# Building a graph's count matrix by ranges of 32 destinations, with paired comparisons and addresses on GpSimd

## The reference, cut to what matters

```
src = randint(40000, 0, 2500)
dst = int(2500 * uniform(40000) ** 2.0)      # then both sorted by dst
W   = zeros((256, 256)).at[src, dst].set(edge_weight)     # second layer; the last writer wins
out = segment_sum(alpha * h[src], dst)                    # attention, and the like for means
```

## Time and profile before

| | us |
|---|---|
| median of 3 runs | 2374.59 (2371.84 to 2375.01) |
| profiled execution, span | 2375.9 |
| counting stage, first to last matmul of line 571 | 41.6 to 335.6 |
| PE busy over the span | 1749.6 |
| VectorE busy | 1671.4 |
| ScalarE busy | 1385.3 |
| GpSimd busy | 334.5 |

### The profile page before, as it was taken

How to read it: one execution, slowest core, us unless ns; L and a number is a source line. 1 busy time by engine, 2 the same in 40 slices (tenths; PEclk the granted TensorE clock), 3 DMA queues, 4 the chain that set the end, 5 groups by cost and what they waited for, 6 DMA issues and landing times. The chain is left out here.

```text
span 2375.9 us, 66901 instructions
## 1 busy us (share of the span) xinstructions
PE 1749.6 (74%) x21978; PEld 1347.5 (57%) x21978; DVE 1671.4 (70%) x3910; ACT 1385.3 (58%) x2252; POOL 334.5 (14%) x547
## 2 busy tenths in 40 slices
PE   3998864488989334998891489994977984288981
PEld 1333323488888224888881356662546983288881
DVE  6988875799999658999997511113332256799997
ACT  0246762899999328999992412122122352599993
POOL 2465301666000012000000000000000000400000
PEclk9999987699999677999996799997997997699996
DMA  1000000100110000110101110000001010000002
GB/s 59 1 2 2 2 10 2 35 31 29 36 36 25 12 2 35 36 36 24 36 25 50 44 39 1 0 0 6 1 0 37 22 54 10 16 21 25 19 19 88
DMA packets 29717, 54.86 MB, mean 23 GB/s; under 512 B 10222, under 2 KB 20820, under 8 KB 29104
## 3 DMA queue, kind: packets, MB, share of 16 engines
q1 hardware_dynamic: 24608, 43.89, 5.6%
q0 software_dynamic: 4880, 7.80, 1.0%
HBM read 43.19 MB, written 8.49 MB: 22 GB/s over the span
## 5 line engine op out<-in xcount | busy, mean ns | idle before, releaser
L1117 PE MATMUL ps<-R,M 128*128 128x132 f16 (+1 forms) x8640 | 810.3, 221 | 268.1 <-DVE M L1030 151.6
L1117 PEld LDWEIGHTS ps<-R,M 128*128 128x128 f16 x8640 | 729.6, 97 | 311.5 <-issue 182.8
L986 ACT ACTIVATE Rm<-rows,cB 128x1280 bf16<-128x1280 f32 (+1 forms) x832 | 884.1, 1153 | 35.3 <-DMA rows<-rowd 17.6
L1125 PE MATMUL ps<-HB,C 128*128 128x66 f16 x6400 | 596.3, 193 | 0.0
L1030 DVE TENSOR_TENSOR M<-Rm,C 128x1280 f16<-128x1280 bf16 (+1 forms) x832 | 554.0, 688 | 54.3 <-ACT Rm L986 47.2
L1125 PEld LDWEIGHTS ps<-HB,C 128*128 128x128 f16 x6400 | 571.7, 97 | 0.0
L1389 PE MATMUL psA<-R,C 128*128 128x512 f16 (+1 forms) x1200 | 255.0, 352 | 96.7 <-POOL ones L1441 41.0
L546 DVE TENSOR_SCALAR ohc<-cells,near 128x1280 f16<-128x1280 f16 x387 | 212.9, 550 | 52.9 <-PE acc L571 49.3
L571 PE MATMUL acc<-ohc,ohl 128*128 128x420 f16 (+1 forms) x1161 | 244.2, 348 | 1.5 <-DVE ohl L548 0.2
L1389 PEld LDWEIGHTS psA<-R,C 128*128 (+1 forms) x1200 | 119.8, 100 | 194.5 <-issue 109.6
L1033 DVE SCALAR_TENSOR_TENSOR M<-rows,cN,C 128x1280 f16<-128x1280 f32 x128 | 197.7, 1545 | 0.0
(11 more groups left out here) (274 smaller groups left out, 2326.5 us busy)
## 6 DMA issues: line engine op xcount, KB each, us to landing
rows<-rowd SPq DMA_DIRECT2D x32, 640.0 KB, 3.9
rows<-rowd SPq DMA_DIRECT2D x16, 320.0 KB, 3.5
xd<-R SPq DMA_DIRECT2D x1, 2560.0 KB, 7.4
xr<-xd SPq DMA_DIRECT2D x20, 128.0 KB, 2.0
xd<-HB SPq DMA_DIRECT2D x1, 2560.0 KB, 9.4
xr<-xd POOLq DMA_DIRECT2D x1, 2560.0 KB, 10.8
R<-in_x SPq DMA_DIRECT2D x1, 2432.0 KB
R<-in_x POOLq DMA_DIRECT2D x1, 2432.0 KB, 10.2
```

Of the source, the lines that this page charges most:

```text
L986: a.activation(Rm[:, s % SG, :], rows[:, p % 2, :], ACT.Relu, bias=cB[:, ds(h + s * nh, 1)]).then_inc(s_R, 1)
L1117: m = pe.matmul(region(p % 2, r), lhsT, rhs, start=first, stop=True, skip_group_check=True)
L1125: m = pe.matmul(both[:, :, cw:2 * cw], C[:, s * NP + p * W + r * P:][:, 0:P], VP[:, s, :, ds(h * cw, cw)], start=False, stop=True, skip_gr ...
```

## The change

It halves the range to 32 destinations (80 ranges, 640 cells in a one-hot). A turn of VectorE's loop now handles two chunks: one tensor_tensor comparison builds both source one-hots, against a copy of b in f16 in which every value stands twice (bpair), and two comparisons build the cell one-hots. There are four buffers of each kind, two for a turn, and which two is computed from the turn's number. PE takes two matmuls for each chunk, 512 and 128 columns, with the buffers' places computed too. A range's sum lies in two banks, and ScalarE copies it in one instruction. Relative codes and the rounds of the search still come once in 64 destinations (NQ = 40). The cells for the scatter are computed by GpSimd at the start of the second phase, no longer by VectorE in the first.

```diff
-WW = 64
+WW = 32
-U3 = 3
+NQ = NW // 2
+U2 = 2
...
+                    if q == 1:
+                        ch(v.tensor_copy(bpair[:, g * P:(g + 1) * P, :], pst[n % 4][:, :].unsqueeze(2).to_broadcast([P, P, 2])))
...
-                ch(v.scalar_tensor_tensor(tmp[:, :], aT[:, :], float(P), bT[:, :], ALU.mult, ALU.add))
-                ch(v.tensor_scalar(wcell[:, :], aT[:, :], float(D // P), None, ALU.is_lt))
-                ch(v.tensor_scalar(late[:, 0:NG * P], dstT[:, :], float(D), None, ALU.is_lt))
...
-                ch(v.memset(late[:, :], 0.0))
...
-                ch(v.tensor_scalar(threes, threes, 1 / U3, 1 / U3, ALU.mult, ALU.add))
+                ch(v.tensor_scalar(pairs, pairs, 1 / U2, 0.5 / U2, ALU.mult, ALU.add))
...
+            BANKS = [(0, 4 * P), (4 * P, CELLS)]
...
+                ch = Chain(g, s_cell)
+                ch(g.tensor_scalar(inside[:, :], aT[:, :], float(D // P), None, ALU.is_lt))
+                ch(g.tensor_scalar(wcell[:, :], dstT[:, :], float(D), None, ALU.is_lt))
+                ch(g.tensor_scalar(cell[:, :], aT[:, :], float(P * D), -float(OOB), ALU.mult, ALU.add))
...
                 last_wins(g, scattering, 0, s_late)
...
+                    for half in range(2):
+                        n = 2 * q + half
+                        done = a.snap(a.to_reg(done + pairs_of(packed(a, n))), min_val=2, max_val=NW * NCH)
+                        hold(a, s_used, done * U2 + 2 * U2)
+                        dest = C[:, :].rearrange("p (s d) -> p s d", d=NP)[:, :, n * WW:(n + 1) * WW]
+                        a.activation(dest, acc[:, half, 0:CELLS].rearrange("p (d s) -> p s d", s=NT),
+                                     ACT.Copy).then_inc(s_out, 1)
...
+            def slots(first_slot):
+                return nc.s_assert_within(first_slot, 0, U2, skip_runtime_bounds_check_because=
+                                          "the remainder by two of a count, times U2")
...
+                    with v.Fori(0, pairs) as i:
+                        at = slots((before + i) % 2 * U2)
+                        k = chunk(first + i * U2, NG * P - U2)
+                        v.wait_ge(s_used, (before + i) * U2 + U2)
+                        v.tensor_tensor(ohl[:, ds(at, U2), :].rearrange("p u (j w) -> p u j w", w=2),
+                                        lows[:, :].rearrange("p (u j w) -> p u j w", u=1, w=2).to_broadcast([P, U2, P // 2, 2]),
+                                        bpair[:, ds(k, U2), :].unsqueeze(2).to_broadcast([P, U2, P // 2, 2]),
+                                        ALU.is_equal).then_inc(s_oh, 1)
+                        for u in range(U2):
+                            v.tensor_scalar(ohc[:, ds(at + u, 1), :], cells[:, half * CELLS:(half + 1) * CELLS].unsqueeze(1),
+                                            near[:, q % 2, ds(k + u, 1)], None, ALU.is_equal).then_inc(s_oh, 1)
...
+                    def pair(i, opening):
+                        at = slots((before + i) % 2 * U2)
+                        for u in range(U2):
                             first_ = opening and u == 0
+                            pe.wait_ge(s_oh, (before + i) * (U2 + 1) + u + 2)
+                            if first_:
+                                pe.wait_ge(s_out, n + 1)
+                            for b0, b1 in BANKS:
+                                ins = pe.matmul(acc[:, half, b0:b1], ohl[:, ds(at + u, 1), :].rearrange("p u j -> p (u j)"),
+                                                ohc[:, ds(at + u, 1), b0:b1].rearrange("p u c -> p (u c)"),
                                                 start=first_, stop=True, skip_group_check=True)
```

More of the change, by code:

```diff
@@ L336, in _ @@
                 ch.wait()
-                first, threes = row[:, 0, :], row[:, 1, :]
+                first, pairs = row[:, 0, :], row[:, 1, :]
                 ch(v.tensor_scalar(first, lh[:, 0, :], -1.0, FAR, ALU.mult, ALU.add))
@@ L436, in build @@
         with Phase() as ph:
-            ohc = ph.sb("ohc", [P, U3, CELLS], f16)
-            ohl = ph.sb("ohl", [P, U3, P], f16)
+            ohc = ph.sb("ohc", [P, 2 * U2, CELLS], f16)
+            ohl = ph.sb("ohl", [P, 2 * U2, P], f16)
+            cell = ph.sb("cell", [P, NG * P], f32)
+            inside = ph.sb("inside", [P, NG * P], f32)
             near = ph.sb("near", [P, 2, NG * P], f32)
@@ L471, in first_of, with pairs_of @@
                                           "the table is built with its first chunk limited to NCH - 1")
-            def threes_of(entry):
+            def pairs_of(entry):
                 return nc.s_assert_within(entry // PACK, 2, NCH, skip_runtime_bounds_check_because=
-                                          "the table is built with at least two threes, and no more than cover NCH chunks")
+                                          "the table is built with at least two pairs, and no more than cover NCH chunks")
             @block.gpsimd
@@ L489, in _ @@
                 turns = turns_of(sp)
-                for q in range(NW):
+                for q in range(NQ):
                     w = q % 2
@@ L536, in _ @@
                 coming, before = packed(v, 0), 0
[L537 to L550, removed]
+                for n in range(NW):
+                    q, half = divmod(n, 2)
+                    first, pairs = first_of(coming), pairs_of(coming)
+                    if n + 1 < NW:
+                        coming = packed(v, n + 1)
+                    if half == 0:
+                        v.wait_ge(s_near, q + 1)
+                    with v.Fori(0, pairs) as i:
[9 more added lines that the diff above has]
+                                            near[:, q % 2, ds(k + u, 1)], None, ALU.is_equal).then_inc(s_oh, 1)
+                    before = v.snap(v.to_reg(before + pairs), min_val=0, max_val=NW * NCH)
@@ L558, in _ @@
                 coming, before = packed(pe, 0), 0
[L559 to L565, removed]
-                            first_ = opening and u == 0
[L567 to L571, removed]
+                for n in range(NW):
+                    q, half = divmod(n, 2)
+                    pairs = pairs_of(coming)
+                    if n + 1 < NW:
+                        coming = packed(pe, n + 1)
+                    def pair(i, opening):
+                        at = slots((before + i) % 2 * U2)
+                        for u in range(U2):
+                            first_ = opening and u == 0
+                            pe.wait_ge(s_oh, (before + i) * (U2 + 1) + u + 2)
[4 more added lines that the diff above has]
+                                                ohc[:, ds(at + u, 1), b0:b1].rearrange("p u c -> p (u c)"),
@@ L584, in _ @@
-                    three(0, True)
-                    with pe.Fori(1, threes) as i:
-                        three(i, False)
-                    before = pe.snap(pe.to_reg(before + threes), min_val=0, max_val=NW * NCH)
+                    if half == 0:
+                        with pe.Fori(0, turns) as i:
+                            r = turns * q + i
+                            pe.wait_ge(s_sq, r + 1)
+                            hold(pe, s_row[q % 2], turns * (q // 2 * 48) + i * 48 + 48)
+                            pe.matmul(psD[q % 2][:, :], big16[:, :], notlater[:, :, :].rearrange("p u j -> p (u j)"),
+                                      start=True, stop=False)
+                            pe.matmul(psD[q % 2][:, :], left[:, q % 2, :], right[:, q % 2, :], start=False,
+                                      stop=True).then_inc(s_D, 1)
@@ L589, in build @@
+                    pair(0, True)
+                    with pe.Fori(1, pairs) as i:
+                        pair(i, False)
+                    before = pe.snap(pe.to_reg(before + pairs), min_val=0, max_val=NW * NCH)
         edge.close()
```

91 lines of the change are left out of this document (42 added, 49 removed).

## The result

The changed kernel takes 2448.59 us (median of 4 runs, 2447.01 to 2452.03), the kernel before 2373.82 beside it: 1.0317 times as long, 95% interval 1.0302 to 1.0331. I had forecast 2391 us and a range of 2330 to 2425. The side was right; the cost is 75 us where I had 17.

What follows compares the result with a forecast made beforehand. It took VectorE's engine as the counting stage's limit, its sequencer after the change: 306 us from 40.3, plus PE's last pair 1 and holding up 5, ends at 352.3 against 335.8, +16.5 us, so 2391 us, range 2330 to 2425.

Steps and rivals of the forecast that it cites:

- VectorE's own pair: Counting loop: VectorE's sequencer needs 1.22 us for each pair of chunks, above the engine's 0.80.
- VectorE's sum: Counting stage on VectorE: 220 pairs at 1.22 us plus 80 changes of range at 0.5, 308 us.
- GpSimd and ScalarE were covered: Beside the counting loop: ScalarE's copies and GpSimd's new 384-column operations, 8 to 13 us, cost 0.
- the tie of the two: Counting stage: PE's sum of 311 us called the same as VectorE's; 5 us added for holding each other up.
- the step "PE": PE's sequencer in the counting stage: 221 us for pairs and loop ends plus 90 for changes of range, 311 us.
- the pair's own term: PE's sequencer in the counting loop: 0.75 us a pair, plus 0.4 for the loop's end in 140 pairs, 221 us.
- the changes of range: PE's sequencer between ranges: 0.68 us in each of 80, 0.9 more in 40 with a round's matmuls, 90 us.
- The second: Rival: PE is slower, 0.9 us a pair before the loop's 0.4, 344 us, end at 376, 2415; chance 0.12.
- The half-way case: Rival: pairs at 0.96 us, PE's addresses partly shared (0.5 a pair), PE ends about 329 us, 2368; chance 0.21.
- Its sign: Counting stage: VectorE waiting for PE for most of its idle time would point to the slower-PE rival.
- the third: Rival: the clock falls; at half clock a pair is 1.07 us on PE, end near 385, 2424; chance 0.08.
- The first, register entries hidden: Rival: VectorE's engine work of 0.80 us a pair counts, stage ends near 255 us, 2295; chance 0.12 in full.

Runs made afterwards that it cites:

- version 4: Changed kernel with fixed buffer places, two pairs to a loop turn, 236 pairs, ranges opened by zero-weight matmuls: 2355.27 us, ratio 0.9923 to the kernel before.
- Version 5: version 4 with VectorE computing its places and looping pair by pair again, PE keeping fixed places: 2430.44 us, ratio 1.0229 to the kernel before.
- version 6: version 4 with PE computing its places and looping pair by pair again, VectorE keeping fixed places: 2491.53 us, ratio 1.0487 to the kernel before.
- experiment 8: Kernel before, ranges of 64 kept, with the pair loop, bpair and four buffers in computed places: 2444.02 us, ratio 1.0291.
- experiment 1: Changed kernel with both count matmuls cut to 128 columns behind a range's first chunk: 2443.40 us, ratio 1.0297 to the kernel before.
- experiment 2: Changed kernel with one more 512-column matmul behind each chunk into a spare PSUM bank: 2444.32 us, ratio 1.0295 to the kernel before.
- experiment 9: Changed kernel with the scatter cells back on VectorE ahead of the loop: 2446.49 us, ratio 1.0314 to the kernel before.

## Why the prediction was wrong

**What held.** The first count matmul at 39.4 us (39.5 forecast); ohc 0.381 us (0.38), ohl 0.293 (0.31); engine work of a pair 0.80 (version 4's shortest step); VectorE's busy time 202 (200); 8 entries of its sequencer a pair, more than 7:

```profile
L565 DVEq FUSED_REGOPS  x440: 75/179/273, 30.3 to 406.9; - x147
...
L570 DVEq FUSED_REGOPS  x440: 80/93/117, 30.8 to 407.3; - x147
...
L570 DVEq ALU_OP  x220: 40/40/52, 31.1 to 407.4; - x110
...
L561 DVEq FUSED_REGOPS  x440: 63/84/93, 30.2 to 407.5; - x147
L561 DVEq COMPARE_BRANCH  x220: 50/56/69, 31.4 to 407.6; - x110
```

(440 + 440 + 220 + 440 + 220 over 220 pairs.) VectorE's own pair, where it waits for nothing but its sequencer, is 1.29 us (75.17 to 76.46) for my 1.22:

```profile
75.17 0.29 DVE L565 TENSOR_TENSOR ohl<-lows,bpair 128x256 f16 x1 [0.55 <-PE acc L595]
75.38 0.68 DVE L570 TENSOR_SCALAR ohc<-cells,near 128x640 f16 x2
76.46 0.29 DVE L565 TENSOR_TENSOR ohl<-lows,bpair 128x256 f16 x1 [0.40 <-issue]
```

Version 5 has 1.22, with a shorter entry at the loop's end (0.040 for 0.093 us). A change of range adds some 0.62 us to VectorE there (1.84 from pair to pair, 76.77 to 78.61) where I had 0.5. So by the rows VectorE's sum is about 220 x 1.29 + 80 x 0.62 = 333 us for my 308; it stayed below PE's, and so this miss did not show in the time. GpSimd and ScalarE were covered: GpSimd idles 121.7 us ahead of its last addition. A sequencer takes the place of the engine as the limit, as argued, but it is PE's, and not the tie of the two that I had.

**What failed: the step "PE", the pair's own term.** The entries of a pair of chunks on PE's sequencer take 1.22 us, and I had put them at 0.75. In the sum I had 0.75 us for a pair's entries and 0.4 for the loop's end in 140 of them, 220 x 0.75 + 140 x 0.4 = 221 us, and 90 for the changes of range. By the rows a pair is 1.22 us without a branch and 1.44 with a taken one, where I had 0.75 and 1.15. The loop runs for 140 pairs and its branch falls through once in each of 80 ranges, so 60 are taken, not the 140 that I had charged: 220 x 1.22 + 60 x 0.22 = 282 us. Of the stage's 370 (39.4 to 409.6) 88 are left for 80 changes, 40 rounds and the waits between the engines, against my 90 and 5. By this subtraction that term was about right, and the pair's was 61 us too small; the forecast was short by 58.

The trace can be sorted as a check, by what lies between the starts of two pairs' weight loads: 80 steps without a branch take 90 us together, 60 with a taken one 90, and 79 over a change of range 190. My terms gave them 60, 69 and 180. So nearly all of the miss lies within the ranges. The same terms give version 6 236 x 1.22 + 156 x 0.22 + 88 = 410 us, of 415.5 measured; its turns are a little shorter (1.35 to 1.39 us) and its changes, with an opening each, longer, so part of that fit is luck.

Inside the pair, the 0.12 us for a further weight load and matmul at computed places was right (experiment 8). What I had nearly left out is what stands between two chunks and before a pair: waits whose value is computed, the slot's remainder, second addresses. I gave them 0.1 us. The second chunk follows 0.45 us behind the first, and the first's two loads explain only 0.24 of that. The rows of one turn, from 57.1 to 58.6 us:

```profile
L595 PEldq FUSED_REGOPS  x5: 42/46/115, 57.3 to 58.0; - x5
...
L595 PEldq ALU_OP  x1: 32/32/32, 57.9 to 57.9; - x1
...
L591 PEldq ALU_OP  x1: 36/36/36, 57.7 to 57.7; - x1
```

With the two entries and the branch of line 611 these are ten entries, whose durations are about 0.7 us of the 1.44. The other half lies between them. For VectorE I had added 0.046 us behind each entry and engine instruction, and came within 0.07 of its pair; for PE I did not do this sum at all, but took "0.6 to 0.7, then 0.1". The Trainium skill (Perfetto Trace Analysis, Sequencer-only Instruction) says that an entry's duration leaves out fetch, decode and the push of semaphores; this trace agrees in so far as 0.7 us lie between ten entries, and does not show what fills them.

**The rivals.** The second, PE slower at 0.9 a pair before the loop's end, was the right mechanism with too small a size; I gave it 0.12 and priced it at 2415. That price had a slip: its own 344 us from 39.5 us on end at 383.5 and not at 376, which is 2422. (The half-way case's 329 us doesn't follow from its terms either: 0.5 us a pair makes PE's sum 256 us, which ends at 296.) Its sign was in the prediction: VectorE waiting mainly for PE, 130 us against 43 on issue. Of the third the sign came and the price did not: the clock fell to 0.67, and what it costs is at most the 4 to 5 us of experiments 1 and 2: at half clock too a pair's 1.07 us of array work stay beneath the sequencer's 1.22 and 1.44. (Only behind a round's matmuls does the array show, with weight loads 0.53 us apart from chunk to chunk: 306.37, 306.91, 307.44.) The first, register entries hidden, is what version 4 makes of the change; there the stage ends at 318.9 us and not at 255. The thin ranges take 4.99 us and not 4.3 (27 of them, 19 us), and 16 pairs were added (some 13 us); the other half of the 64 us I have not divided.

## What to carry to other kernels

This is what the case suggests for others. In a loop whose instructions are short, price each engine by its sequencer first: entries and the gaps behind them, for PE as carefully as for VectorE, and the waits with computed values too. A ring of buffers wants as many copies of the body in a turn as there are places, so that places are constants; padding the trips to fit (236 pairs for 220) cost far less than computing them. A halved tile pays only when the engine, and not its sequencer, is the limit.

## What the hardware showed

- 440 weight loads and as many matmuls at fixed places, put among entries that compute, cost PE's sequencer nothing measurable (experiment 2: 2444.3 us, against 2443.4 in experiment 1 at the same clock), while two more of each at computed places cost 0.24 us a pair (experiment 8).
- The granted clock did not simply follow the amount of work here: with 281 us of PE's listed work in the stage it was 0.67, with 228 us (fewer columns to a matmul, the same number of matmuls) it was 1.00, and with 281 us at nearly twice the columns 1.00 again. These are listed times, longer at half clock. Why the version with the fewest columns kept the full clock stays open.
- Beside GpSimd's new chain of 384-column operations (40.8 to 52.6 us) VectorE's instructions ran longer: at first 0.40 to 0.45 us for ohl in place of 0.29, and 0.91 to 2.23 in place of 0.68 for two cell one-hots. With the chain taken away (experiment 9) they took 0.29 and 0.68 from the first of these pairs on.
